# FFN: the block scales of h computed on VectorE ahead of the inverse, instead of on GpSimd

## What is computed

```python
BLOCK = 16
def fp4_quant_dequant(x):
    xb = x.reshape(shape[:-1] + (shape[-1] // BLOCK, BLOCK))
    scale = jnp.max(jnp.abs(xb), axis=-1, keepdims=True) / 6.0
    scale = jnp.maximum(scale, jnp.float32(1e-12))
    xn = xb / scale
    idx = jnp.searchsorted(_MID, jnp.abs(xn))
    q = _GRID[idx] * jnp.sign(xn) * scale
...
gate = fp4_linear(x, w_gate)
y = fp4_linear(x, w_up)
h = jax.nn.silu(gate) * y
return fp4_linear(h, w_down)
```

## Time and profile before

| | |
|---|---|
| median of three runs | 577.37 us |
| the profiled execution: its time, its span | 577.54 us, 575.6 us |
| TensorE matmuls busy | 558.3 us (97%) |
| VectorE busy | 514.5 us (89%) |
| ScalarE busy | 363.9 us (63%) |
| GpSimd busy | 239.5 us (42%) |
| L1373 (h_scale on GpSimd) | 31 times, 0.36 us each |

### The profile page before, as it was taken

One profiled execution on the slowest core, in us unless ns is written; L12 is line 12 of the kernel. 1 busy time (PEld: TensorE's weight loads), 2 busy tenths in 40 slices (PEclk: granted clock), 3 DMA queues, 4 the chain that ended last, 5 costly groups with the idle time before them and its releaser, 6 DMA issues.

```text
span 575.6 us, 14088 instructions
## 1 busy us (share of the span) xinstructions
PE 558.3 (97%) x4408; PEld 482.1 (84%) x4408; DVE 514.5 (89%) x1193; ACT 363.9 (63%) x931; POOL 239.5 (42%) x291
## 2 busy tenths in 40 slices
PE   7999999999999999999999999999999999999993
PEld 4788888888888888888888788889999989999983
DVE  7667878999999999899999889999999999999996
ACT  4455766777686676777668654556555766676563
POOL 2211121534435344343534323665665665665430
PEclk9999999999999999999999999999999999999998
DMA  7611110110111011011001000000000110010013
GB/s 210 225 35 32 56 47 12 56 54 1 54 55 34 21 55 46 9 55 55 27 27 36 19 11 10 1 0 2 2 1 2 38 38 2 19 38 20 2 36 109
DMA packets 24984, 22.31 MB, mean 39 GB/s; under 512 B 2026, under 2 KB 21875, under 8 KB 24947
## 3 DMA queue, kind: packets, MB, share of 16 engines
q1 hardware_dynamic: 24130, 20.27, 11.4%
q10 hardware_dynamic: 816, 1.57, 0.8%
HBM read 17.63 MB, written 4.20 MB: 38 GB/s over the span
## 4 chain that ended last, share of the span: by engine, by line
PE 71%; DVE 18%; issue 5%; POOL 2%; DMA 2%; ACT 1%; DVEq 0%; ACTq 0%; POOLq 0%
PE wide_banks L1415 40%; PE wide_banks L1486 9%; PE wide_banks L1631 5%; PE wide_banks L1463 4%; DVE shared L891 3%; PE wide_banks L1474 3%; PE turn L1512 3%; PE turn L1449 2%; DVE h_amax L875 2%; DVE shared L1121 2%; PE wide_banks L1499 2%; PE wide_banks L1603 2%; DVE win_lo L1008 2%; POOL shared L1368 1%; DVE shared L896 1%
## 5 line engine op out<-in xcount | busy, mean ns | idle before, releaser
L1379 POOL TENSOR_TENSOR shared<-shared,h_scale 128x704 f32<-128x704 bf16 x31 | 43.0, 1389 | 81.9 <-DVE shared L896 79.4
L1415 PE MATMUL wide_banks<-win_hi,x_hi 128*128 128x512 f32 x192 | 65.5, 422 | 3.1 <-DVE shared L711 1.5
L1486 PEld LDWEIGHTS wide_banks<-shared 128*128 128x128 f32 x512 | 62.0, 192 | 2.8
L484 ACT ACTIVATE shared<-opened,rstd 128x64 f32<-128x64 f32 x240 | 63.5, 339 | 1.1
L1415 PE MATMUL wide_banks<-wgu_hi,xq_hi 128*128 128x512 f32 (+1 forms) x192 | 60.2, 395 | 1.4 <-DVE xq_lo L1113 1.3
L1486 PE MATMUL wide_banks<-shared 128*128 128x64 f32 x512 | 60.6, 271 | 0.0
L1415 PE MATMUL wide_banks<-win_hi,x_lo 128*128 128x512 f32 x192 | 60.3, 395 | 0.0
L1415 PE MATMUL wide_banks<-win_lo,x_hi 128*128 128x512 f32 x192 | 60.3, 395 | 0.0
L1415 PE MATMUL wide_banks<-wgu_lo,xq_hi 128*128 128x512 f32 (+1 forms) x192 | 56.5, 375 | 0.0
L1415 PE MATMUL wide_banks<-wgu_hi,xq_lo 128*128 128x512 f32 (+1 forms) x192 | 56.4, 375 | 0.0
L450 ACT ACTIVATE shared<-shared 128x704 bf16<-128x704 f32 x32 | 25.3, 789 | 44.9 <-POOL shared L1368 43.4
(11 more groups left out here) (156 smaller groups left out, 1472.3 us busy)
## 6 DMA issues: line engine op xcount, KB each, us to landing
xf<-in_x_feat SPq DMA_DIRECT2D x32, 128.0 KB, 2.2
tab<-in_tables SPq DMA_DIRECT2D x16, 256.0 KB, 2.7
xt<-in_x_tok SPq DMA_DIRECT2D x32, 128.0 KB, 2.1
out<-x SPq DMA_DIRECT2D x32, 128.0 KB, 1.7
x<-in_w_in ACTq DMA_DIRECT2D x3, 512.0 KB, 5.3
w<-in_w_gu SPq DMA_DIRECT2D x1, 1408.0 KB, 7.7
w<-in_w_down SPq DMA_DIRECT2D x1, 704.0 KB, 8.9
wgu_lo<-pow_dram SPq DMA_DIRECT2D x1, 576.0 KB, 4.8
```

Source lines behind the costliest of these rows:

```text
L484: last = act.activation(gated[:, b, cols], opened[:, b, cols], ACT.Copy, scale=rstd[:, b, 1 + k:2 + k])
L1379: pool.tensor_tensor(over_blocks(hq[:, b]), over_blocks(h_steps[:, b]), spread(h_fp4["scale"][:, b]), ALU.mult).then_inc(h_fp4["ready"], 1)
L1415: last = pe.matmul(dst, lhs, rhs, start=k == 0, stop=k == len(parts) - 1)
L1486: last = pe.matmul(mixed[:, r, DV * at:DV * (at + 1)], ret[:, slot(k)], vs[:, b, DV * k:DV * (k + 1)], start=False, stop=k >= HEADS - 2, s ...
```

## The change

`h_scale` for tiles 0 to 30 is taken off GpSimd and done on VectorE, as for tile 31: ahead of the step that leads to the inverse, both from the same maxima. The semaphore `h_scaled` goes: L875 no longer waits for GpSimd, since the readers of the maxima are now on its own engine, and `rescale_h` no longer waits for it either, since it waits for `rounded`, which VectorE signals later in its order. The new step waits on `h_fp4["ready"]`, which says that the buffer of the scale two tiles back has been used.

```diff
-        h_shifted, h_scaled = sem("h_shifted"), sem("h_scaled")
+        h_shifted = sem("h_shifted")
...
             def h_max(n):
-                need(dve, h_scaled, n)
                 dve.tensor_reduce(h_fp4["amax"][:], over_blocks(h[:, n % 2]), AX.X, ALU.max, apply_absolute_value=True).then_inc(h_fp4["step"], 1)
 
             def h_scale(n, b):
+                need(dve, h_fp4["ready"], n - 1)
                 dve.wait_ge(h_fp4["step"], H_STEPS * n + 1)
-                if n == TILES - 1:
-                    dve.wait_ge(h_fp4["ready"], n - 1)
-                    dve.tensor_scalar(h_fp4["scale"][:, b], h_fp4["amax"][:], 1.0 / FP4_MAX, SCALE_MIN, ALU.mult, ALU.max)
+                dve.tensor_scalar(h_fp4["scale"][:, b], h_fp4["amax"][:], 1.0 / FP4_MAX, SCALE_MIN, ALU.mult, ALU.max)
                 dve.tensor_scalar(h_fp4["inv"][:], h_fp4["amax"][:], -TIE_DOWN / FP4_MAX, -SCALE_MIN * TIE_DOWN,
                                   ALU.mult, ALU.min).then_inc(h_fp4["step"], 1)
...
-            def h_scale(n, b):
-                pool.wait_ge(h_fp4["step"], H_STEPS * n + 1)
-                need(pool, h_fp4["ready"], n - 1)
-                pool.tensor_scalar(h_fp4["scale"][:, b], h_fp4["amax"][:], 1.0 / FP4_MAX, SCALE_MIN, ALU.mult, ALU.max).then_inc(h_scaled, 1)
-
             def rescale_h(n, b):
                 need(pool, hT_done, n - 1)
-                pool.wait_ge(h_scaled, n + 1)
                 pool.wait_ge(h_fp4["rounded"], n + 1)
...
-                if valid(n - 1) and n < TILES:
-                    h_scale(n - 1, 1 - b)
```

## The result

| | before | after |
|---|---|---|
| median of 12 runs each | 577.38 us (577.06 to 577.90) | 578.36 us (577.99 to 579.92) |
| ratio, 95% interval | | 1.0019 (1.0012 to 1.0026) |
| profiled execution: time, span | 577.54, 575.6 us | 578.24, 576.2 us |

I had forecast 576.6 us and a range up to 578.3. The difference is about the size of what a measurement can tell, but its interval leaves out 1, and its sign is not the forecast one. The spans of the 12 runs of after lie between 576.1 and 576.6 us, and before has only one here, 575.6.

What follows compares the result with a forecast made beforehand. VectorE was taken to set the pace to about body 18, TensorE after; h_scale's price and the roundings' gains summed to -0.88 us, plus 0.12 for a later L1368, about -0.8: 576.6 us, range 575.8 to 578.3.

Steps and rivals of the forecast that it cites:

- What bounds the kernel: In the 32 feed-forward bodies, VectorE sets the pace to about body 18, then TensorE at 6.74 us each.
- The price of h_scale: On VectorE between L875 and L882, 31 times: the added operation costs 0.09 us per body, bounds 0.05 to 0.17.
- The roundings: In eight bodies GpSimd's rounding of x starts earlier without L1373 before it; each body gets 0.35 us shorter.
- the last term of the sum: In six norm-step bodies up to 15, GpSimd's L1368 comes about 0.02 us later each, +0.12 us in all.
- My three signs of being wrong: In the changed profile: h_inv lasting 0.6 us, L1362 growing over 0.1 us, or held L891 keeping its 1.70 us.
- The ledger: Summed shifts of VectorE's L1113 against before: -0.34 us at body 6, -0.41 at body 15, -1.02 at body 18.
- The range: Measured time between 575.8 and 578.3 us, holding the forecast, no effect, cheaper and full price; chance 0.81.
- Third held: In norm-step bodies the third small VectorE operation may come too late, costing 0.47 us; 578.9 us, chance 0.07.

Runs made afterwards that it cites:

- the memsets alone: Changed kernel with 24 one-column memsets added at VectorE's start, into columns of out_mean so no buffer moves; 578.31 us, 1.0010 of the kernel before.

## Why the prediction was wrong

**What bounds the kernel** held. The end moved by what L1113 did up to body 15, less the 0.44 us that TensorE makes good, and in every kernel but the one with the scale twice the transposes of the bodies from 24 to 29 came at TensorE's own pace, 6.74 or 6.77 us.

**The price of h_scale**, 0.09 us taken over from body 32, was nearly right: 0.07. The difference is GpSimd's L1371, which now starts 0.11 us before the body instead of 0.08 and lets go as much sooner. The kernels without the wait for h_scaled all show the 0.11 us, the one that kept it (only GpSimd's order changed) has 0.08.

**The roundings** gave 0.48 to 0.50 us each instead of 0.35. I had taken 0.44 us away, L1373's 0.36 and one gap of 0.08. But there had been a second gap of about 0.09 between L1368 and L1373, and now the rounding starts with none at all behind L1366: it moved up by 0.50 against the body's start.

**The step that failed** is the last term of the sum, "L1368 about 0.02 us later in each of the six bodies with a norm step". I had the other outcome as a rival, with a chance of 0.07: it happened in every one of the six, at 0.36 to 0.39 us each over the price of the same body without a norm step. (The rival itself counted five; it left out body 5.) What led me wrong was how I read the earlier trace rows. L1052 beside L1362, unheld, I took as proof that VectorE keeps the port while its operations overlap. What it proves is less: an operation that starts together with L1362 still comes through. The third one starts 0.09 us later, and by then L1362 has the port. The rule of the Trainium skill that I had cited, from the page "SBUF — State Buffer" (section "Who interferes with whom"), says just this (whoever issues first has it for the whole instruction), and I weighed it against the second operation, where the trace could answer, and passed over the third, where it could not. My three signs of being wrong had the same blind spot, and none of them came: h_inv took 0.17 us, L1360 grew to 0.66, and the held L889 fell to 1.15.

The ledger up to L1111 of body 15, in measured terms: -0.19 (this execution began its first body so much earlier), +0.13 for bodies 1 to 3, -0.62 for 4 and 5, +1.23 for 6 and 7, +0.11 for 8 and 9, -0.97 for 10 and 11, +0.92 for 12 to 14, +0.45 for 15's own: +1.06, less the 0.02 in hand, against 1.03 seen. The forecast for the same place was -0.41, ahead of the last term. The six held steps are 6 x 0.37 = 2.2 of the difference, the wait in body 7 is 0.36 (the trace of before has nothing that shows it), and the better roundings, the cheaper h_scale and the earlier start take some 1.1 back.

**The range** went wrong with the chances. "Third held" alone would have been 578.9 by my prices, outside the range. As measured it is less: with the memsets alone, where the steps are held and body 7 has no wait, the kernel took 0.54 us more than before, which would be 577.9 us here (an estimate from that run). So the held steps turned the sign, and it took the wait in body 7 as well, which I could not have seen, to put the time 0.06 us above the range. A rival whose only refutation is a row for a neighbouring case deserved more than 0.07.

## What to carry to other kernels

Count VectorE's small operations that stand in a row behind one that is held by GpSimd. In this kernel the first pays the hold, the second comes through by a hundredth of a microsecond (in two variants it failed to in one body each), and the third, 0.09 us later, waits until GpSimd's next instruction is nearly over, unless it is of a kind that isn't held. Before moving work from GpSimd to VectorE, look at what it stands in front of on GpSimd, since changing the order there may give the whole gain (0.9968) at no price. A row that shows an operation unheld proves it only for its own start against the other engine's.

## What the runs showed that I had not expected

- A wait of 0.46 us between two operations of VectorE, at the same instruction in the changed kernel and five variants of it, which goes away when 24 instructions are put in at the program's start, and shows only where 1655 instructions stand ahead of it. That it is the loading of code is my guess; no row shows what the engine waited for.
- 96 bytes more of buffer per partition, with nothing written to them, slow TensorE's feed-forward body from 6.74 to 6.77 us, and make the median span 576.9 us where the same kernel without them has 576.7 (on another chip; the kernel before has 575.8 on both). Which of the tensors behind the buffer matters was not tried.
- Reciprocals (0.16 to 0.19 us long) are not held by GpSimd in a place where `tensor_scalar`, `tensor_tensor` and `scalar_tensor_tensor` are.
- Two waits ahead of an instruction cost 0.07 us more in one order (the one already met first) than in the other: 0.98 against 0.91 us.
